# Attention: the product with the values in two halves of the queries, one behind each pair of score banks

## The chip, the cores and the metric

The kernel runs on one core of a Trainium2 chip. The metric is the device time of one execution in microseconds (us), the median of several; smaller is better. TensorE does the matrix products, VectorE (DVE) the reductions, ScalarE (ACT) the exponentials and copies, GpSimd (POOL) the masking of probabilities, and SyncE (SP) issues the transfers.

## What is computed

One transformer layer on x of shape 4 x 2048 x 256 in f32: causal attention with 16 heads of 16, then an MLP with ternary weights. The change touches the attention alone. Cut to that:

```python
def _L0_attn_ref(x, W_attn, b_attn, W_proj, b_proj):
    qkv = x @ W_attn + b_attn
    q, k, v = jnp.split(qkv, 3, axis=2)
    qh, kh, vh = (heads(q), heads(k), heads(v))          # b h s d, d = 16
    scores = jnp.einsum('bhqd,bhkd->bhqk', qh, kh) * scale
    causal = jnp.tril(jnp.ones((S, S), dtype=bool))
    scores = jnp.where(causal, scores, -jnp.inf)
    probs = jax.nn.softmax(scores, axis=-1)
    out = jnp.einsum('bhqk,bhkd->bhqd', probs, vh)
    out = out.transpose(0, 2, 1, 3).reshape(B, S, D)
    return out @ W_proj + b_proj

x = x + _L0_attn_ref(_layernorm(x), ...)
x = x + _L0_ffn_ref(_layernorm(x), ...)
```

## The kernel before

Four parts follow each other: build_prep (weights), build_qkv (norm and q, k, v to DRAM), build_attention, build_mlp. The attention takes the time from about 290 to 1763 us of the span and is the only part that changes.

**Units and steps.** A unit is one batch and one group of four heads; there are 16. In a unit the queries go in four chunks of 512. STEPS lists the work of a unit: in chunk c, 4c + 1 steps of one block (128 keys by 512 queries), then a double-block step (384 and 128 queries, two different key blocks at the diagonal), then a two-bank step (256 queries, two heads side by side in a bank). That makes 36 steps, 32 with four banks of scores (one a head) and 4 with two. Diagonal blocks are masked.

**What a step does.** TensorE writes the scores of a bank into `ps_s` (L961), a ring of three PSUM banks (BANKS = 3). A head pair lies in two row groups of the array: banks 0 and 2 use partitions 0 to 49 (r = 0), banks 1 and 3 partitions 64 to 113 (r = 1). ScalarE takes the exponential of each bank into `probs` (L848), a ring of six steps in SBUF. Three steps later (PV_BEHIND = 3) TensorE multiplies them with the values into `ps_acc` (L980), the four heads in four column groups of 32; each f32 product is two records in the trace, so a step's product shows as x8. The last matmul of a step's product signals pv_done; at the end of a chunk ScalarE copies `ps_acc` (L831) and signals acc_copied.

**Maxima.** The maximum of each query is needed as an extra row of q before its scores. It is found ahead of time (LEAD = 40 items): an item is a pair of matmuls into `ps_m` (L926), one in each row group, and one reduction on VectorE (L871, L874); there are two slots (SLOTS = 2). A unit has 68 items. Of the 20 at the diagonal, 8 have four mask products each and 12 have eight (L932, bf16, 128 columns). Once a chunk the maxima are parted on POOL (L774, L776), turned on TensorE into a bank of the ring (L939), copied on ScalarE (L823) and sent by SP into q.

**What sets the order.** Each engine runs its instructions in the order written, and `order(s, last)` (L112) lists the pieces of step s for all engines: banks, items, the turn ("rows") and the product ("values"). TensorE alone takes the "values" pieces from it. `await_bank` (L942) makes the scores of ring use k wait until ScalarE has read use k - 3. `values` (L965) waits for the masks of its step (L971) or its exponentials (L973), and at a chunk's start for the copy of the accumulator (L976).

Of the kernel before, what the change touches and what calls it, by code (L numbers as in the profile page):

```python
# [64 lines left out]
STEPS = [step for c in range(NCH) for step in  # L65
         [(c, 1, [(j, 0, 0, CH)]) for j in range(TT * c + 1)]
         + [(c, 1, [(TT * c + 1, P, 0, 3 * P), (TT * c + 3, 3 * P, 3 * P, P)]), (c, 2, [(TT * c + 2, 2 * P, 0, 2 * P)])]]
NS = len(STEPS)
CHUNK_END = [s + 1 for s in range(NS) if s + 1 == NS or STEPS[s + 1][0] > STEPS[s][0]]
CHUNK_START = [0] + CHUNK_END[:-1]  # L70
DIAGONALS = [s for s, (c, _, blocks) in enumerate(STEPS) if blocks[0][0] >= TT * c]
ND = len(DIAGONALS)
PV_BEHIND = 3


def banks_of(s):

    return GH // STEPS[s][1]
# [17 lines left out]
def items_at(x):  # L96

    y = x + LEAD  # L100
    got = [("item", (y >= NM, y % NM))]
    for what, z in (("found", y - 1), ("rows", y - ROWS_BEHIND)):
        if z >= 0 and z % NM + 1 in MAX_END:
            got.append((what, (z >= NM, MAX_END.index(z % NM + 1))))
    return got
# [6 lines left out]
def order(s, last):  # L112


    x = sum(banks_of(i) // 2 for i in range(s))
    if banks_of(s) == 4:
        got = [("bank", 0), ("bank", 1), *items_at(x), ("bank", 2), ("values", None), ("bank", 3), *items_at(x + 1)]
    else:
        got = [("bank", 0), ("bank", 1), ("values", None), *items_at(x)]
    return [(what, y) for what, y in got if not (last and what in ("item", "found", "rows") and y[0])]  # L120


def ring_uses(s, last):
# [15 lines left out]
def zero(n):  # L139

    return isinstance(n, int) and n == 0
# [460 lines left out]
def build_attention(nc, io, keep, scr):  # L602

    with ExitStack() as ctx:
# [26 lines left out]
        pv_done, loads_passed = t.sem("pv_done"), t.sem("loads_passed")  # L631
# [20 lines left out]
        def uses(n, u, by):  # L652

            return by * (n // 2 + 1) if isinstance(n, int) else by // 2 * (n + 2 - u)

        def halves(n, c):

            return 2 * n + c // 2
# [9 lines left out]
        def taken(n, k):  # L668

            return OPENED_ROWS + USES * n + k + 1  # L670
# [6 lines left out]
        def unit_of(x, n, u):  # L677

            return n + 1 if x[0] else n, 1 - u if x[0] else u, x[1]
# [232 lines left out]
        @block.tensor  # L912
        def _(pe):
            def form_max(n, par, k):
                c, pieces = MAXES[k]
                slot = k % SLOTS
                if not (isinstance(n, int) and NM * n + k < SLOTS):

                    pe.wait_ge(slot_freed, NM * n + k - SLOTS + 1)
                if k in [0] + MAX_END:  # L920

                    pe.wait_ge(stack_in[par][c], uses(n, par, 16 * STACK))
                for p, tt, i, col, width in pieces:
                    for r in range(2):
                        rows = slice(ROW * r, ROW * r + TERMS)
                        last = pe.matmul(ps_m[:, 2 * slot + r, col:col + width], qs[par][rows, c, p, tt * P:(tt + 1) * P],  # L926
                                         ks[par][rows, i, p, 0:width], start=True, stop=(i < c), skip_group_check=True)
                    if i == c:
                        for half in range(2):
                            for r in range(2):  # L930
                                rows = slice(ROW * r, ROW * (r + 1))
                                last = pe.matmul(ps_m[:, 2 * slot + r, col + width - P:col + width], ident_half[rows, half],  # L932
                                                 mask_half[rows, half], start=False, stop=(half == 1), skip_group_check=True)
                last.then_inc(slot_filled, 1)

            def turn_rows(n, c, k):

                pe.wait_ge(max_parted, 2 * NCH * n + 2 * (c + 1))
                pe.transpose(ps_s[0:MROWS * GH * TT, k % BANKS, 0:P],  # L939
                             max_parts[c % 2][:].bitcast(F32).rearrange("p r a x -> p (r a x)"), keep["ident"][:]).then_inc(ring_filled, 1)  # L940

            def await_bank(n, k, first):  # L942

                if k >= BANKS:
                    pe.wait_ge(ring_taken, taken(n, k - BANKS))
                elif not first:
                    pe.wait_ge(ring_taken, taken(n, -1 - (USES - 1 - k) % BANKS))
                elif k < OPENED_ROWS:
                    pe.wait_ge(ring_taken, k + 1)

            def scores(n, u, s, bank, k):
                c, heads, blocks = STEPS[s]
                if s in CHUNK_START and bank == 0:

                    pe.wait_ge(rows_in[c % 2], 16 * 2 * MROWS * (halves(n, c) + 1))
                for x in range(heads):
                    p, r = (bank + 2 * x) // 2, bank % 2
                    rows = slice(ROW * r, ROW * r + TERMS + MROWS)
                    for j, q0, col, width in blocks:
                        at = CH // heads * x + col  # L960
                        last = pe.matmul(ps_s[:, k % BANKS, at:at + width], ks[u][rows, j // TT, p, j % TT * P:(j % TT + 1) * P],  # L961
                                         qs[u][rows, c, p, q0:q0 + width], start=True, stop=True, skip_group_check=True)
                last.then_inc(ring_filled, 1)

            def values(n, u, s, last_unit):  # L965
                c, heads, blocks = STEPS[s]
                if s == 0:
                    pe.wait_ge(v_in[u], uses(n, u, 16))
                if s in DIAGONALS:
                    before = sum(len(STEPS[i][2]) for i in DIAGONALS if i <= s)  # L970
                    pe.wait_ge(probs_masked, MASKS * n + before)  # L971
                else:
                    pe.wait_ge(ring_taken, scores_taken(n, s, last_unit))  # L973
                if s in CHUNK_START and not (zero(n) and c == 0):

                    pe.wait_ge(acc_copied, NCH * n + c)  # L976
                for j, q0, col, width in blocks:
                    for h in range(GH):
                        at = h // banks_of(s) * (CH // heads) + col
                        last = pe.matmul(ps_acc[h * VW:(h + 1) * VW, q0:q0 + width], vs[u][:, j, h],  # L980
                                         probs[:, s % RING, h % banks_of(s), at:at + width],
                                         start=(j == 0), stop=(s + 1 in CHUNK_END), skip_group_check=True)
                last.then_inc(pv_done, 1)

            MASKS = sum(len(STEPS[i][2]) for i in DIAGONALS)
            pe.wait_ge(fixed_in, 16 * FIXED)
            opened = 0
            for what, x in OPENING:
                if what == "item":
                    form_max(0, 0, x[1])  # L990
                elif what == "rows":
                    turn_rows(0, x[1], opened)
                    opened += 1

            def body(n, u, first, last):
                k = 0
                for s in range(NS):
                    for what, x in order(s, last):
                        if what == "bank":
                            await_bank(n, k, first)  # L1000
                            scores(n, u, s, x, k)
                            k += 1
                        elif what == "item":
                            form_max(*unit_of(x, n, u))
                        elif what == "rows":
                            unit, _, c = unit_of(x, n, u)
                            await_bank(n, k, first)
                            turn_rows(unit, c, k)
                            k += 1
                        elif what == "values" and s >= PV_BEHIND:  # L1010
                            values(n, u, s - PV_BEHIND, last)
                        elif what == "values" and not first:
                            values(n - 1, 1 - u, NS + s - PV_BEHIND, False)
                if last:
                    for s in range(NS - PV_BEHIND, NS):
                        values(n, u, s, True)

            over_units(pe, body)


# [286 lines left out]
```

## Time and profile before

| | |
|---|---|
| median of 3 runs | 2255.41 us (2251.96 to 2268.09) |
| profiled execution | 2259.07 us, its span 2257.1 us |
| TensorE busy | 2076.8 us, 92% |
| VectorE busy | 1845.8 us, 82% |
| ScalarE busy | 1441.3 us, 64% |
| POOL busy | 469.2 us, 21% |

Shares of busy time are means over all four parts of the program. A matmul's end in the trace is modelled and matmuls overlap, so TensorE's busy share is no measure of how full it is; the distance between the starts of its instructions is. Times in the rows below are from the span's start.

### The profile page before, as it was taken

How to read it: one execution, taken by the hardware profiler on the slowest of the kernel's cores; microseconds unless marked ns; L12 is line 12 of the kernel's file. 1: busy time of each engine (PE TensorE's matmuls, PEld its weight loads, DVE VectorE, ACT ScalarE, POOL GpSimd, SP SyncE). 2: the span in 40 equal slices, each digit the busy share in tenths (PEclk: the TensorE clock that was granted, in tenths of full speed). 3: DMA queues.
4: the chain of work that ended last, by engine and by line, in shares of the span. 5: the costliest groups of instructions: out<-in, count | busy, mean ns of one | idle time of the engine just before them, and what ended most of it. 6: DMA issues, size and time to landing. Idle time of an engine off the chain costs nothing. (4 is left out here: it accounts for less than half of the span.)

```text
span 2257.1 us, 40453 instructions
## 1 busy us (share of the span) xinstructions
PE 2076.8 (92%) x15605; PEld 1216.2 (54%) x15605; DVE 1845.8 (82%) x2413; ACT 1441.3 (64%) x2768; POOL 469.2 (21%) x621
## 2 busy tenths in 40 slices
PE   3997699999999999999999999999999488888888
PEld 2886354444544545444444454454543277777777
DVE  7896888888888888888888888888881288787776
ACT  1332078787888878878888788787887243444444
POOL 0000011111110111101111111011110256666664
PEclk8998589999999999999999999999998599999999
DMA  2899321222222122222122212211210212222220
GB/s 90 325 372 333 66 47 54 68 62 57 59 61 75 44 54 68 58 68 51 54 65 58 63 53 66 75 45 54 67 41 11 89 45 69 75 75 75 75 75 29
DMA packets 162976, 184.69 MB, mean 82 GB/s; under 512 B 41936, under 2 KB 102880, under 8 KB 160736
## 3 DMA queue, kind: packets, MB, share of 16 engines
q1 hardware_dynamic: 154112, 174.50, 26.0%
q10 hardware_dynamic: 8672, 7.60, 1.1%
q8 instruction: 123, 2.02, 0.4%
q14 instruction: 69, 0.57, 0.1%
HBM read 104.16 MB, written 76.02 MB: 80 GB/s over the span
## 5 line engine op out<-in xcount | busy, mean ns | idle before, releaser
L848 ACT ACTIVATE probs<-ps_s 128x512 f32<-128x512 f32 x2176 | 1144.5, 602 | 302.8 <-PE ps_s L961 293.1
L871 DVE TENSOR_REDUCE maxes<-ps_m 128x2 f32<-128x1024 f32 (+1 forms) x960 | 1136.8, 1218 | 160.2 <-PE ps_m L926 105.9
L961 PE MATMUL ps_s<-qs,ks 50*128 50x512 f32 (+3 forms) x2560 | 805.9, 414 | 9.0 <-ACT probs L848 9.0
L926 PE MATMUL ps_m<-ks,qs 48*128 48x512 f32 (+3 forms) x2560 | 715.5, 426 | 35.0 <-DMA ks<-ones 23.9
L961 PEld LDWEIGHTS ps_s<-qs,ks 50*128 50x128 f32 x2560 | 402.8, 188 | 505.4 <-ACT probs L848 464.6
L980 PE MATMUL ps_acc<-probs,vs 128*32 128x512 f32 (+3 forms) x5120 | 594.3, 546 | 0.6
L926 PEld LDWEIGHTS ps_m<-ks,qs 48*128 48x128 f32 x2560 | 362.5, 190 | 125.1 <-issue 44.8
L786 POOL TENSOR_SCALAR_AFFINE_SELECT probs<-probs 128x512 f32<-128x512 f32 x256 | 157.0, 635 | 746.1 <-ACT probs L848 746.1
L1119 POOL TENSOR_TENSOR hid<-square,hid 128x512 fp32r<-128x512 f32 x128 | 196.2, 1554 | 184.7 <-DVE square L1144 174.4
L932 PE MATMUL ps_m<-mask_half,ident_half 64*128 64x128 bf16 x2048 | 207.3, 227 | 0.0
L980 PEld LDWEIGHTS ps_acc<-probs,vs 128*32 128x32 f32 x5120 | 109.2, 109 | 159.8 <-issue 94.2
L874 DVE TENSOR_REDUCE maxes<-ps_m 128x2 f32<-128x768 f32 (+1 forms) x256 | 161.7, 685 | 28.7 <-PE ps_m L932 28.2
L1144 DVE TENSOR_TENSOR square<-relu 128x512 f32<-128x512 f32 x128 | 134.9, 1074 | 58.5 <-ACT relu L1178 55.5
L1241 PE MATMUL ps_y<-w,hid 128*128 128x256 f32 x1024 | 140.8, 299 | 1.5 <-POOL hid L1119 1.4
L774 POOL CAST max_parts<-neg_max 128x16 fp32r<-128x16 f32 x64 | 12.6, 196 | 606.1 <-DVE neg_max L880 606.1
L1241 PEld LDWEIGHTS ps_y<-w,hid 128*128 128x128 f32 x1024 | 135.9, 206 | 2.2 <-POOL hid L1119 2.1
L1178 ACT ACTIVATE relu<-ps_h 128x512 f32<-128x512 f32 x128 | 76.2, 595 | 68.0 <-PE ps_h L158 59.0
L156 PE MATMUL ps_h<-mxn_t,w 128*128 128x512 f32 x256 | 105.2, 411 | 2.5 <-DVE mxn_t L434 1.4
L157 PE MATMUL ps_h<-mxn_t,w 128*128 128x512 f32 x256 | 103.3, 404 | 0.0
L932 PEld LDWEIGHTS ps_m<-mask_half,ident_half 64*128 64x128 bf16 x2048 | 94.7, 98 | 15.5 <-issue 5.5
L158 PE MATMUL ps_h<-mxn_t,w 128*128 128x512 f32 x256 | 101.8, 398 | 0.0
L1183 ACT ACTIVATE hid<-relu 128x512 fp32r<-128x512 f32 x128 | 81.0, 633 | 4.0
(126 smaller groups left out, 1589.6 us busy)
## 6 DMA issues: line engine op xcount, KB each, us to landing
qs<-q_scr SPq DMA_DIRECT2D x384, 64.0 KB, 2.7
ks<-k_scr SPq DMA_DIRECT2D x384, 64.0 KB, 2.7
q_scr<-parts SPq DMA_DIRECT2D x32, 512.0 KB, 4.0
k_scr<-parts SPq DMA_DIRECT2D x32, 512.0 KB, 5.5
v_scr<-v_out SPq DMA_DIRECT2D x16, 1024.0 KB, 7.4
vs<-v_scr SPq DMA_DIRECT2D x16, 1024.0 KB, 5.9
o_scr<-acc_sb SPq DMA_DIRECT2D x64, 256.0 KB, 2.9
o_in<-o_scr SPq DMA_DIRECT2D x32, 256.0 KB
```

What stands on the lines that cost most here:

```text
L156: pe.matmul(out, sh, mh, start=start, stop=False)
L786: pool.affine_select(out=tile, in_=tile, compare_op=ALU.is_ge, fill=0.0, base=0, pattern=[[0, GH], [1, P]], channel_multiplier=-1).then_in ...
L848: act.activation(probs[:, s % RING, x], ps_s[:, k % BANKS], ACT.Exp).then_inc(ring_taken, 1)
L871: last = dve.tensor_reduce(maxes[c % 2][:, :, pairs, tt, i], banks, AX.X, ALU.max)
L874: last = dve.tensor_reduce(maxes[c % 2][:, :, p, tt, i], ps_m[:, 2 * slot:2 * slot + 2, col:col + width], AX.X, ALU.max)
L926: last = pe.matmul(ps_m[:, 2 * slot + r, col:col + width], qs[par][rows, c, p, tt * P:(tt + 1) * P], ks[par][rows, i, p, 0:width], start=T ...
L932: last = pe.matmul(ps_m[:, 2 * slot + r, col + width - P:col + width], ident_half[rows, half], mask_half[rows, half], start=False, stop=(h ...
L961: last = pe.matmul(ps_s[:, k % BANKS, at:at + width], ks[u][rows, j // TT, p, j % TT * P:(j % TT + 1) * P], qs[u][rows, c, p, q0:q0 + widt ...
L980: last = pe.matmul(ps_acc[h * VW:(h + 1) * VW, q0:q0 + width], vs[u][:, j, h], probs[:, s % RING, h % banks_of(s), at:at + width], start=( ...
L1119: pool.tensor_tensor(hid[:, 1, m], square[:, m], hid[:, 0, m].bitcast(F32), ALU.subtract).then_inc(low_done, 1)
L1144: dve.tensor_tensor(square[:, m], relu[:, m], relu[:, m], ALU.mult).then_inc(square_done, 1)
L1241: last = pe.matmul(ps_y[:, i, (tt % 2) * DIM:(tt % 2 + 1) * DIM], hid[:, a, m, tt * P:(tt + 1) * P], keep["w2"][:, m], start=(m == 0 and a ...
```

## The change

In a four-bank step the order was: bank 0, bank 1, an item, bank 2, the product, bank 3, an item. It becomes: bank 0, bank 1, an item, the first half of the product, bank 2, bank 3, an item, the second half. The halves part the queries: 256 and 256 of a plain step's 512, 128 and 128 of a two-bank step's 256, and the 384 and the 128 of a double-block step. In a two-bank step both halves stand where the product stood. The waits stand before the first half, and pv_done is signalled by the second.

```diff
@@ order
     if banks_of(s) == 4:
-        got = [("bank", 0), ("bank", 1), *items_at(x), ("bank", 2), ("values", None), ("bank", 3), *items_at(x + 1)]
+        got = [("bank", 0), ("bank", 1), *items_at(x), ("values", 0), ("bank", 2), ("bank", 3), *items_at(x + 1), ("values", 1)]
     else:
-        got = [("bank", 0), ("bank", 1), ("values", None), *items_at(x)]
+        got = [("bank", 0), ("bank", 1), ("values", 0), ("values", 1), *items_at(x)]
...
+def halves_of(s):
+
+    blocks = STEPS[s][2]
+    j, q0, col, width = blocks[0]
+    if len(blocks) > 1:
+        return [blocks[:1], blocks[1:]]
+    return [[(j, q0, col, width // 2)], [(j, q0 + width // 2, col + width // 2, width // 2)]]
...
-            def values(n, u, s, last_unit):
-                c, heads, blocks = STEPS[s]
-                if s == 0:
+            def values(n, u, s, half, last_unit):
+                c, heads, _ = STEPS[s]
+                if s == 0 and half == 0:
                     pe.wait_ge(v_in[u], uses(n, u, 16))
-                if s in DIAGONALS:
+                if half == 0 and s in DIAGONALS:
                     before = sum(len(STEPS[i][2]) for i in DIAGONALS if i <= s)
                     pe.wait_ge(probs_masked, MASKS * n + before)
-                else:
+                elif half == 0:
                     pe.wait_ge(ring_taken, scores_taken(n, s, last_unit))
-                if s in CHUNK_START and not (zero(n) and c == 0):
+                if half == 0 and s in CHUNK_START and not (zero(n) and c == 0):
 
                     pe.wait_ge(acc_copied, NCH * n + c)
-                for j, q0, col, width in blocks:
+                for j, q0, col, width in halves_of(s)[half]:
                     for h in range(GH):
                         at = h // banks_of(s) * (CH // heads) + col
                         last = pe.matmul(ps_acc[h * VW:(h + 1) * VW, q0:q0 + width], vs[u][:, j, h],
                                          probs[:, s % RING, h % banks_of(s), at:at + width],
-                                         start=(j == 0), stop=(s + 1 in CHUNK_END), skip_group_check=True)
-                last.then_inc(pv_done, 1)
+                                         start=(j == 0 and half == 0), stop=(s + 1 in CHUNK_END), skip_group_check=True)
+                if half == 1:
+                    last.then_inc(pv_done, 1)
```

On TensorE a plain step (512 columns everywhere) read like this before; `ps_s` are scores, `ps_m` an item, `ps_acc` the product.

```order
L961 MATMUL ps_s<-qs,ks 128x512
L926 MATMUL ps_m<-ks,qs 128x512 x2
L961 MATMUL ps_s<-qs,ks 128x512 x2
L926 MATMUL ps_m<-ks,qs 128x512 x2
L961 MATMUL ps_s<-qs,ks 128x512
L980 MATMUL ps_acc<-probs,vs 32x512 x4
```

And now, the same step:

```order
L970 MATMUL ps_s<-qs,ks 128x512 x2
L935 MATMUL ps_m<-ks,qs 128x512 x2
L989 MATMUL ps_acc<-probs,vs 32x256 x4
L970 MATMUL ps_s<-qs,ks 128x512 x2
L935 MATMUL ps_m<-ks,qs 128x512 x2
L989 MATMUL ps_acc<-probs,vs 32x256 x4
```

The scores of bank 3 (the first row of before) have moved up beside those of bank 2, and each pair is followed by an item and half a product.

The end of a chunk on TensorE, from the product of the last four-bank step over the two-bank step (`128x256 x4`) to the next chunk, before:

```order
L980 MATMUL ps_acc<-probs,vs 32x512 x4
L961 MATMUL ps_s<-qs,ks 128x384
L961 MATMUL ps_s<-qs,ks 128x128
L926 MATMUL ps_m<-ks,qs 128x256 x2
L932 MATMUL ps_m<-mask_half,ident_half 128x128 x4
L926 MATMUL ps_m<-ks,qs 128x256 x2
L932 MATMUL ps_m<-mask_half,ident_half 128x128 x4
L961 MATMUL ps_s<-qs,ks 128x256 x4
L980 MATMUL ps_acc<-probs,vs 32x512 x4
L926 MATMUL ps_m<-ks,qs 128x512 x2
L961 MATMUL ps_s<-qs,ks 128x512 x2
```

And now:

```order
L970 MATMUL ps_s<-qs,ks 128x384
L970 MATMUL ps_s<-qs,ks 128x128
L970 MATMUL ps_s<-qs,ks 128x384
L970 MATMUL ps_s<-qs,ks 128x128
L935 MATMUL ps_m<-ks,qs 128x256 x2
L941 MATMUL ps_m<-mask_half,ident_half 128x128 x4
L935 MATMUL ps_m<-ks,qs 128x256 x2
L941 MATMUL ps_m<-mask_half,ident_half 128x128 x4
L989 MATMUL ps_acc<-probs,vs 32x256 x4
L970 MATMUL ps_s<-qs,ks 128x256 x4
L989 MATMUL ps_acc<-probs,vs 32x256 x8
L935 MATMUL ps_m<-ks,qs 128x512 x2
```

The item with its eight mask products now stands between the pieces of a whole pair of scores and half a product, and in the two-bank step the halves touch (x8).

## Rows read from the trace of the kernel before

**Rows 1.** The page's busy times (us, share of the span, instructions).
```profile
PE 2076.8 (92%) x15605; PEld 1216.2 (54%) x15605; DVE 1845.8 (82%) x2413; ACT 1441.3 (64%) x2768; POOL 469.2 (21%) x621
```

**Rows 2.** Windows view, one unit: us; busy of PE, PEld, DVE, ACT, POOL; clock; DMA.
```profile
836.60:928.50 91.90, 91.64 (x775) 44.57 (x772) 81.51 (x85) 73.89 (x145) 11.45 (x24) 1.00 0.21 60
```

**Rows 3.** Timeline of ScalarE, copies a unit apart: start, length, line, operation, shapes, count, idle.
```profile
849.99 0.60 ACT L848 ACTIVATE probs<-ps_s 128x512 f32<-128x512 f32 x1
850.48 0.58 ACT L831 COPY acc_sb<-ps_acc 128x512 f32<-128x512 f32 x1
...
942.33 0.58 ACT L831 COPY acc_sb<-ps_acc 128x512 f32<-128x512 f32 x1
```

**Rows 4.** Groups by form in one unit (836.6 to 928.5): busy us, mean ns, idle before.
```profile
L871 DVE TENSOR_REDUCE maxes<-ps_m 128x2 f32<-128x1024 f32 x57 | 67.6, 1218 | 8.2 <-PE ps_m L926 7.2 <-PE ps_m L932 0.8
...
L932 PE MATMUL ps_m<-mask_half,ident_half 64*128 64x128 bf16 x128 | 13.0, 222 | 0.0
```

**Rows 5.** Timeline of TensorE in a plain step.
```profile
908.35 1.06 PE L980 MATMUL ps_acc<-probs,vs 128*32 128x512 f32 x8
909.35 0.50 PE L961 MATMUL ps_s<-qs,ks 50*128 50x512 f32 x1
909.35 0.73 PE L926 MATMUL ps_m<-ks,qs 48*128 48x512 f32 x2
...
909.93 0.63 PE L926 MATMUL ps_m<-ks,qs 48*128 48x512 f32 x2
910.53 0.49 PE L961 MATMUL ps_s<-qs,ks 50*128 50x512 f32 x1
910.96 1.06 PE L980 MATMUL ps_acc<-probs,vs 128*32 128x512 f32 x8
```

**Rows 6.** Timeline of ScalarE: the exponential of the scores of 909.35.
```profile
909.88 0.60 ACT L848 ACTIVATE probs<-ps_s 128x512 f32<-128x512 f32 x1 [0.54 <-PE ps_s L961]
```

**Rows 7.** Timeline of TensorE behind a two-bank step's product.
```profile
859.35 0.50 PE L926 MATMUL ps_m<-ks,qs 48*128 48x512 f32 x2
859.69 0.40 PE L961 MATMUL ps_s<-qs,ks 50*128 50x512 f32 x2
859.92 0.39 PE L926 MATMUL ps_m<-ks,qs 48*128 48x512 f32 x2
860.16 0.39 PE L961 MATMUL ps_s<-qs,ks 50*128 50x512 f32 x1
860.47 1.07 PE L980 MATMUL ps_acc<-probs,vs 128*32 128x512 f32 x8
```

**Rows 8.** Timeline of TensorE in a two-bank step, up to its product.
```profile
857.41 0.44 PE L961 MATMUL ps_s<-qs,ks 50*128 50x384 f32 x1
...
857.75 0.68 PE L961 MATMUL ps_s<-qs,ks 50*128 50x256 f32 x4
858.36 0.64 PE L980 MATMUL ps_acc<-probs,vs 128*32 128x512 f32 x4
```

**Rows 9.** Timeline of TensorE: a product of 256 columns and the next scores.
```profile
848.88 0.64 PE L980 MATMUL ps_acc<-probs,vs 128*32 128x256 f32 x8
849.45 0.50 PE L961 MATMUL ps_s<-qs,ks 50*128 50x512 f32 x1
```

**Rows 10.** Timeline of TensorE: ends of two stretches with masked items.
```profile
872.06 0.50 PE L961 MATMUL ps_s<-qs,ks 50*128 50x512 f32 x1
...
873.75 1.06 PE L980 MATMUL ps_acc<-probs,vs 128*32 128x512 f32 x8
...
877.60 0.50 PE L961 MATMUL ps_s<-qs,ks 50*128 50x512 f32 x1
...
879.46 1.06 PE L980 MATMUL ps_acc<-probs,vs 128*32 128x512 f32 x8
```

**Rows 11.** Timeline of TensorE: a stretch with a turn of the maxima.
```profile
887.89 0.49 PE L926 MATMUL ps_m<-ks,qs 48*128 48x512 f32 x2
...
889.43 0.64 PE L980 MATMUL ps_acc<-probs,vs 128*32 128x512 f32 x4
```

More of the change, by code:

```diff
@@ L1010, in body @@
                         elif what == "values" and s >= PV_BEHIND:
-                            values(n, u, s - PV_BEHIND, last)
+                            values(n, u, s - PV_BEHIND, x, last)
                         elif what == "values" and not first:
-                            values(n - 1, 1 - u, NS + s - PV_BEHIND, False)
+                            values(n - 1, 1 - u, NS + s - PV_BEHIND, x, False)
                 if last:
                     for s in range(NS - PV_BEHIND, NS):
-                        values(n, u, s, True)
+                        for half in range(2):
+                            values(n, u, s, half, True)
             over_units(pe, body)
```

## The prediction

> **What bounds the kernel now.** The page comes first: TensorE is busy for 92% of the span [rows 1]. The windows view of one unit of attention says more: VectorE works 81.51 of 91.90 us and ScalarE 73.89, while the 91.64 of TensorE count overlapping, modelled matmuls as busy [rows 2], so that number can't tell a full TensorE from one that waits. A unit lasts 91.85 us, from one copy of the accumulator (L831) to the same copy a unit later [rows 3]; 16 units are 1470 of the 2257.1 us. VectorE's 67.6 us of large reductions in a unit [rows 4] leave it some 10 us short of the unit: it is the next bound, not this one.
>
> The timeline of a plain step (four banks, two plain items) shows the bound [rows 5]. From product (908.35) to product (910.96) it takes 2.61 us. The product itself holds TensorE 1.00 us (908.35 to 909.35). The stretch from there to the next product is 1.61. In it the scores of bank 2 start at 910.53, 0.60 after the matmuls of 909.93, where others start 0.23 apart. They wait for ScalarE: ring slot k takes the scores of k, and k-3 must have been read. For bank 2 that is bank 3 of the step before, whose scores began at 909.35, whose exponential began at 909.88 and took 0.60 [rows 6]. So there is a loop: scores of bank 3, exponential, scores of bank 2 (1.18 to 1.19 later), 0.42 to the product, 1.00 of product, scores of bank 3 again: 2.61. How long would the stretch be without it? The stretch after a two-bank step has seven matmuls of 512 columns, in four slots of paired row groups as a plain step has, and takes 1.12 [rows 7]. The wait is thus worth 1.61 - 1.12 = 0.49 in a plain step.
>
> **A ledger of the unit before.** It has 32 four-bank and 4 two-bank steps. Content without waits: 32 stretches of 1.12; four of 0.95, that of a two-bank step (857.41 to 858.36) [rows 8]; 32 products of 1.00 and 4 of 256 columns at 0.57 [rows 9]. Masks: 128 mask products in a unit [rows 4], in 12 items of eight and 8 of four by the code. A stretch with two items of eight takes 1.86 (877.60 to 879.46), one with an eight and a four 1.69 (872.06 to 873.75) [rows 10]; against 1.12 this is 0.37 for an item of eight and 0.20 for one of four. Turning the maxima (L939) makes a stretch 1.54 (887.89 to 889.43) [rows 11], 0.42 more, four times. Sum: 35.8 + 3.8 + 32.0 + 2.3 + 4.4 + 1.6 + 1.7 = 81.6. The unit takes 91.85, so 10.2 us are waits, nearly all the one above. That is also where masks hide now: a stretch with one item of four has 1.32 of content and fits under 1.61.
>
> **What the change does, part by part.**
>
> 1. Bank 2 and bank 3 are now neighbours, and half a product stands after each pair. The half cycle is: scores pair, item, half product. The first pair after a product takes 0.34 to the next, the last 0.31 to the product (859.35 to 859.69, 860.16 to 860.47) [rows 7]: 0.65. Half a product is the 256-column one, 0.57 [rows 9]. Sum 1.22, a plain step 2.44. Does the ring allow it? The second score of a pair now needs the exponential of the first score of the pair before: the same 1.19, against 1.22. The wait is gone with 0.03 to spare. A plain step gains 0.17.
> 2. The price in every step: splitting a product costs 2 x 0.57 - 1.00 = 0.14, and going from scores to product and back twice costs 2 x 0.65 - 1.12 = 0.18. In the two-bank steps the halves touch, and the split costs 0.05 (0.14 less the 0.09 of one switch). First the row: the first pair after a product needs 0.34 where others need 0.23 [rows 7]. The Trainium skill (TensorEngine Tiling (Array Packing), Key Properties) says that changing the tiling mode drains the engine; scores use row groups and the product column groups, so this rule speaks against the change. It gives no figure. Were the drain free, the 32 x 0.18 = 5.8 us of a unit would go; I keep them, since both sides of the 256-column product show the full switch.
> 3. Stretches: the 64 half cycles have 60 x 0.65, and 4 after a two-bank step 0.88 (one more pair, 0.23); the two-bank stretches 4 x 0.71 (its four pieces to the product 0.61 [rows 8], and 0.10 for being first): 45.3. Products: 34.3 + 32 x 0.14 + 4 x 0.05 = 39.0. The second product half signals pv_done, and ScalarE's ring of six steps is three away: nothing.
> 4. Masks 6.0 and turns 1.7 as before, but now with no wait to hide in: the spare is 0.03 a half.
> 5. Scores in pieces: each of the four double-block steps has 4 pieces in place of a pair, twice. Bounds: 0 (hidden in the other row group) and 0.30 (four pieces 0.61 [rows 8] against a pair 0.31). I take 0.20: 8 x 0.20 = 1.6.
> 6. New waits. A half with a 128-column product (0.57 - 0.21 = 0.36, by the 0.43 that 256 columns cost) lasts 1.01 and then waits for the ring until 1.19: 0.18, some 6 times without masks, 1.1. The copy of the accumulator: the last half of a chunk's last product now ends a step, ScalarE copies it behind the exponential of bank 3 (0.58 for the copy [rows 3]), and the next chunk's first half comes one half cycle later, not one step: scores of that step at 1.01 after bank 2's, product wanted at 1.66, copy done at 0.53 + 2 x 0.49 (one exponential or copy to the next [rows 3]) + 0.58 = 2.1. That is 0.5 once, and where masks lengthen the half some 0.1: 0.7 together. A turn takes a ring slot between two pairs, so that bank 3 waits for the exponential of bank 1: 0.15 x 4 = 0.6. Bounds of all: 0.5 and 4.
>
> POOL's masks and SP's queue keep their order; the product waits for masks three steps old. VectorE is busy 81.51 for the 68 items of a unit [rows 2], 1.20 an item, against halves of 1.22 and more: it still hides, and is late next if the halves get shorter.
>
> Sum after: 45.3 + 39.0 + 6.0 + 1.7 + 1.6 + 2.4 = 96.0 us, against 91.85: **+4.1 a unit, +66 in 16 units**. The profiled execution has 2259.07 us, the median is 3.7 below: 2325 less 4, **about 2320 us**, 2.9% slower. In short: 0.17 is won in the plain steps, fewer than half of all, and each masked step of two eights goes from 2.86 to 2.44 + 0.74 = 3.18.
>
> **Rivals.** The forecast has 66%.
>
> A, faster: what is hidden today stays hidden. An all-plain unit would take 32 x 2.61 and four times 0.95 + 1.12 + 0.57 - 1.61 = 1.03, that is 87.6 us, so masks, turns and pieces add only 4.2 today. If that stays, the unit is 84.3 + 4.2 = 88.5 (84.3 is the first two sums of step 3), and the kernel 2255 - 54 = 2201. It turns at 91.85 - 84.3 = 7.5 us of exposed extras; I count 11.7. For it: two row groups run side by side. Against it: the unstalled 1.86 of two masked items [rows 10]. 12%.
>
> B, within 1%: masks cost their streaming alone. A pair of 512 columns takes 0.23, so a pair of mask products (128 columns) 0.06: 0.24 and 0.12 for items of eight and four, 3.8 a unit and not 6.0; then 93.8, +31. With the pieces free as well (bound 0), 92.2: +6, 2261. The Trainium skill (the same section) has different tiles execute weight loads and matmuls in parallel, which is this case; rows 10 show no sign of it where the loads are many. 16%, around 2270.
>
> C, much slower: the 0.03 of spare isn't there. If the second score of a pair loads its weights late, 0.1 in each of some 44 unmasked halves is 4.4 a unit, 70 more: 2390. 6%.
>
> At the bounds of the terms: if the new waits are at 4 and the pieces at 0.30, the unit is 98.4 and the kernel 2360. It is the upper end of the forecast's own 66%, of which most lies between 2285 and 2352.
>
> The edit can hardly fail to do what it says, since the order on TensorE is written out.
>
> **Numbers.** Range 2256 to 2352: it holds the forecast and B, and leaves out A, C and the outermost of the bounds. A change of 1% is 22.5 us, about what a measurement can tell. Faster by over 1%: A, 0.12. Within: B, 0.16. Slower: the forecast and C, 0.72.
>
> **What would show it.** Plain steps of 2.44 between like halves, without the 0.60 gap before scores: step 1. Half products 0.57 apart from the next scores: step 2. Stretches of scores and an item of eight at 1.02: step 4. A gap of half a microsecond before the first product of a chunk: step 6. A unit (copy to copy) of 96.0. I am wrong if plain steps stay at 2.6 (C), or masked halves are about as short as plain ones (A).

## The result, and the profile after

| | before | after |
|---|---|---|
| median us, 20 runs each | 2262.49 (2249.91 to 2276.22) | 2276.94 (2260.49 to 2288.98) |
| ratio, 95% interval | | 1.0061 (1.0031 to 1.0090) |
| profiled execution, its span | 2259.07, 2257.1 | 2287.96, 2286.2 |
| one unit, copy to copy | 91.87 | 92.98 |

The kernel became slower by 0.6%, about 14 us, where 2.9%, some 65 us, were forecast. The sign was right, the size more than four times too large.

The unit is the better measure: within one execution it repeats to 0.1 us in most units (those of the changed kernel behind the first lie between 93.0 and 93.8), while whole executions of either kernel scatter by over 1%. Two copies of the accumulator, one unit apart, from ScalarE's timeline after the change (before: [rows 3]):

```profile
1323.45 0.57 ACT L840 COPY acc_sb<-ps_acc 128x512 f32<-128x512 f32 x1
...
1416.43 0.57 ACT L840 COPY acc_sb<-ps_acc 128x512 f32<-128x512 f32 x1
```

16 units of +1.1 us are +18 us, inside the interval of the ratio (7 to 20 us). The two profiled executions differ by 29; 7 of the other 11 us lie in the first unit, where the granted clock was 0.50 of full in one execution and 1.00 in the other. The windows view of 300 to 315 us, of before:

```profile
300.00:315.00 15.00, 15.00 (x115) 6.51 (x114) 13.49 (x14) 12.19 (x25) 2.44 (x4) 1.00 0.45 80
```

and of after (the clock is the third number from the end):

```profile
300.00:315.00 15.00, 15.00 (x96) 5.81 (x96) 7.35 (x6) 7.34 (x14) 2.49 (x4) 0.50 0.38 80
```

Executions of one and the same kernel differ in the granted clock as well: twenty of the changed kernel had means over the span from 0.945 to 0.960, and took 2289 us at the lower and 2260 at the higher. So these 7 us aren't put down to the change. One execution of each kernel was profiled, so whether the clock always differs at this place isn't shown.

**A plain step**, TensorE's timeline after, which answers to [rows 5]:

```profile
927.73 0.64 PE L989 MATMUL ps_acc<-probs,vs 128*32 128x256 f32 x8
928.30 0.51 PE L970 MATMUL ps_s<-qs,ks 50*128 50x512 f32 x2
928.64 0.40 PE L935 MATMUL ps_m<-ks,qs 48*128 48x512 f32 x2
928.98 0.64 PE L989 MATMUL ps_acc<-probs,vs 128*32 128x256 f32 x8
929.54 0.50 PE L970 MATMUL ps_s<-qs,ks 50*128 50x512 f32 x2
929.88 0.40 PE L935 MATMUL ps_m<-ks,qs 48*128 48x512 f32 x2
930.21 0.64 PE L989 MATMUL ps_acc<-probs,vs 128*32 128x256 f32 x8
```

From 927.73 to 930.21 it takes 2.48 us, against 2.61. The gap of 0.60 before the scores of bank 2 is gone. Half a product holds TensorE 0.57 (927.73 to 928.30), the pair and the item 0.67 (928.30 to 928.98).

**Masked items.** Two halves with items of eight mask products, which answer to [rows 10]:

```profile
882.65 0.50 PE L970 MATMUL ps_s<-qs,ks 50*128 50x512 f32 x2
...
883.17 0.29 PE L941 MATMUL ps_m<-mask_half,ident_half 64*128 64x128 bf16 x4
...
883.64 0.64 PE L989 MATMUL ps_acc<-probs,vs 128*32 128x256 f32 x8
884.21 0.50 PE L970 MATMUL ps_s<-qs,ks 50*128 50x512 f32 x2
```

The stretch is 0.99 (882.65 to 883.64), 0.32 more than the plain 0.67; a half is 1.56 and two are 3.11, where such a step took 2.86. What the plain steps win is lost here. With an item of four the stretch is 0.80, 0.13 more:

```profile
888.67 0.50 PE L970 MATMUL ps_s<-qs,ks 50*128 50x512 f32 x2
...
889.47 0.64 PE L989 MATMUL ps_acc<-probs,vs 128*32 128x256 f32 x8
```

**The chunk's start**, with the copy of the accumulator:

```profile
863.34 0.43 PE L989 MATMUL ps_acc<-probs,vs 128*32 128x128 f32 x8
863.70 0.58 PE L970 MATMUL ps_s<-qs,ks 50*128 50x512 f32 x2
...
864.84 0.64 PE L989 MATMUL ps_acc<-probs,vs 128*32 128x256 f32 x8 [0.32 <-ACT acc_sb L840]
```

The stretch is 1.14 instead of 0.67: the first product of the chunk waits for ScalarE's copy.

**The two-bank step** ([rows 8]) and **a turn of the maxima** ([rows 11]):

```profile
871.93 0.50 PE L970 MATMUL ps_s<-qs,ks 50*128 50x256 f32 x4
872.37 1.07 PE L989 MATMUL ps_acc<-probs,vs 128*32 128x256 f32 x16
873.37 0.50 PE L935 MATMUL ps_m<-ks,qs 48*128 48x512 f32 x2
...
874.27 0.64 PE L989 MATMUL ps_acc<-probs,vs 128*32 128x256 f32 x8
...
894.71 0.50 PE L970 MATMUL ps_s<-qs,ks 50*128 50x512 f32 x2
...
895.36 0.29 PE L948 MATMUL ps_s<-ident,max_parts 128*32 128x128 f32 x1
895.58 0.64 PE L989 MATMUL ps_acc<-probs,vs 128*32 128x256 f32 x8
```

The four pieces of the two-bank step are at the product in 0.44; two touching halves take 1.00, as much as the whole product did. This turn stands in a four-bank step, directly ahead of a half product; its stretch is 0.87, 0.20 more than a plain one. So it is for two of the four turns of a unit. The other two belong to two-bank steps and stand between an item and scores, as all four did before:

```profile
902.84 0.49 PE L935 MATMUL ps_m<-ks,qs 48*128 48x512 f32 x2
903.26 0.28 PE L948 MATMUL ps_s<-ident,max_parts 128*32 128x128 f32 x1
903.48 0.50 PE L970 MATMUL ps_s<-qs,ks 50*128 50x512 f32 x2
...
904.15 0.64 PE L989 MATMUL ps_acc<-probs,vs 128*32 128x256 f32 x8
```

This stretch is 1.31, where the same one without a turn takes 0.90 (873.37 to 874.27): 0.40 more. And a double-block step's scores in pieces, 0.72 to the product:

```profile
898.82 0.51 PE L970 MATMUL ps_s<-qs,ks 50*128 50x384 f32 x4
899.17 0.45 PE L935 MATMUL ps_m<-ks,qs 48*128 48x512 f32 x2
899.54 0.64 PE L989 MATMUL ps_acc<-probs,vs 128*32 128x256 f32 x8
```

### The profile page after: what moved, and what is told of

Its sections match the earlier page's. It is cut to its first block and busy times, and to the rows that moved or that the text cites. A ratio compares the mean times of both kernels' runs of the same rounds, so it can differ in the third digit from the quotient of the medians.

```text
span 2286.2 us, 48645 instructions
## 1 busy us (share of the span) xinstructions
PE 2103.6 (92%) x19701; PEld 1175.8 (51%) x19701; DVE 1870.6 (82%) x2413; ACT 1478.3 (65%) x2768; POOL 470.9 (21%) x621
## 5 line engine op out<-in xcount | busy, mean ns | idle before, releaser
L857 ACT ACTIVATE probs<-ps_s 128x512 f32<-128x512 f32 x2176 | 1181.3, 596 | 296.4 <-PE ps_s L970 272.5
L880 DVE TENSOR_REDUCE maxes<-ps_m 128x2 f32<-128x1024 f32 (+1 forms) x960 | 1151.3, 1221 | 157.0 <-PE ps_m L935 98.3
L989 PE MATMUL ps_acc<-probs,vs 128*32 128x256 f32 (+2 forms) x9216 | 711.2, 386 | 11.7 <-ACT acc_sb L840 11.1
L970 PE MATMUL ps_s<-qs,ks 50*128 50x512 f32 (+3 forms) x2560 | 577.2, 454 | 0.0
L935 PE MATMUL ps_m<-ks,qs 48*128 48x512 f32 (+3 forms) x2560 | 525.3, 401 | 35.4 <-DMA ks<-ones 24.3
L970 PEld LDWEIGHTS ps_s<-qs,ks 50*128 50x128 f32 x2560 | 253.1, 188 | 420.1 <-ACT probs L857 392.1
L989 PEld LDWEIGHTS ps_acc<-probs,vs 128*32 128x32 f32 x9216 | 190.9, 109 | 306.6 <-issue 201.0
L935 PEld LDWEIGHTS ps_m<-ks,qs 48*128 48x128 f32 x2560 | 263.5, 192 | 78.7 <-DVE maxes L880 29.8
L941 PE MATMUL ps_m<-mask_half,ident_half 64*128 64x128 bf16 x2048 | 147.3, 227 | 0.0
L941 PEld LDWEIGHTS ps_m<-mask_half,ident_half 64*128 64x128 bf16 x2048 | 63.0, 98 | 71.6 <-issue 66.6
```

Of the source, the lines that this page charges most:

```text
L857: act.activation(probs[:, s % RING, x], ps_s[:, k % BANKS], ACT.Exp).then_inc(ring_taken, 1)
L880: last = dve.tensor_reduce(maxes[c % 2][:, :, pairs, tt, i], banks, AX.X, ALU.max)
```

## The experiments

**Theory 1** is the prediction's: before, a plain step waited for the ring loop, and that wait hid masks, turns and pieces; the change ends the wait and exposes them, and adds switches. **Theory 2**: halves cost by their split and switches alone, masks weigh the same in both kernels. **Theory 3**: TensorE or VectorE, and not the ring, set the plain step before. **Theory 4**: it is the pairing of the scores that shortens the step, the halves only cost. Unit lengths are medians over the units between the same copies of the profiled execution; ratios are to the kernel before on the same chip.

| run | unit us | median us | ratio (95%) |
|---|---|---|---|
| e1 before, no mask products | 89.75 | 2228.79 | 0.9857 (0.9793 to 0.9921) |
| e2 after, no mask products | 89.56 | 2218.56 | 0.9787 (0.9732 to 0.9843) |
| e3 split only | 92.07 | 2266.45 | 1.0013 (0.9976 to 1.0049) |
| e4 mixture | 91.59 | 2245.58 | 0.9917 (0.9882 to 0.9952) |
| e5 before, half exponentials | 89.07 | 2220.03 | 0.9776 (0.9731 to 0.9822) |
| e6 after, half exponentials | 91.44 | 2244.45 | 0.9884 (0.9836 to 0.9932) |
| e7 after, copy early | 93.13 | 2276.57 | 1.0036 (1.0005 to 1.0066) |
| e8 mixture 2 | 91.43 | 2255.97 | 0.9936 (0.9904 to 0.9968) |
| e9 whole product between | 101.13 | 2416.47 | 1.0654 (1.0573 to 1.0736) |
| e10 mixture 3 | 90.82 | 2236.25 | 0.9887 (0.9826 to 0.9948) |

### Are the masks what is exposed? (e1, e2)

The same edit on the kernel before (e1) and on the changed one (e2), in form_max:

```diff
-                                         ks[par][rows, i, p, 0:width], start=True, stop=(i < c), skip_group_check=True)
-                    if i == c:
+                                         ks[par][rows, i, p, 0:width], start=True, stop=True, skip_group_check=True)
+                    if False:
```

> The kernel before, without the mask products (L932) in the items of maxima; the maxima then run over whole blocks, everything else is the same. Theory 1 (what the ring wait of ScalarE hid in the kernel before, the masks above all, is exposed by the change): only what masked stretches last beyond 1.61 us goes, about 2.2 us a unit: unit 91.86 -> about 89.7, time some 35 us less. Theory 2 (the two halves cost by their split and second switch alone, masks weigh the same in both kernels): the masks' whole 4.8 us goes from here too: unit about 87.

> The changed kernel, without the mask products of the maxima. Theory 1: all of the masks' time goes (12 x 0.315 + 8 x 0.13 = 4.8 us a unit, less some ring waits that come back): unit 93.0 -> about 88.5, and so this kernel is faster than the kernel before without masks, by some 1.2 us a unit or 19 us. Theory 2: it stays about 1.1 us a unit slower than the kernel before without masks.

Measured: 91.87 to 89.75 in the kernel before, 2.1 us a unit, as theory 1 had it. In the changed kernel 93.0 to 89.6, 3.4 us. So the masks weigh 1.3 us a unit more in the changed kernel, and without them the change no longer slows a unit: 89.56 against 89.75. More than that can't be read from the two, as the units of e2 lie between 89.1 and 90.3. Theory 1's sign holds, theory 2 falls. The size was off: 4.5 was expected in e2. The masks had covered waits there as well. The chunk start of e2 at 749 us:

```profile
747.35 0.58 PE L970 MATMUL ps_s<-qs,ks 50*128 50x512 f32 x2
...
748.49 0.64 PE L989 MATMUL ps_acc<-probs,vs 128*32 128x256 f32 x8 [0.32 <-ACT acc_sb L840]
```

This stretch of 1.14 now stands at three chunk starts of a unit. In the changed kernel the second of them held an item of four and took 1.03, and the third an item of eight and took about the 0.99 of any such stretch.

### Does the split cost by itself? (e3)

```diff
-        got = [("bank", 0), ("bank", 1), *items_at(x), ("values", 0), ("bank", 2), ("bank", 3), *items_at(x + 1), ("values", 1)]
+        got = [("bank", 0), ("bank", 1), *items_at(x), ("bank", 2), ("values", 0), ("values", 1), ("bank", 3), *items_at(x + 1)]
```

> One part alone: the order of the kernel before, with the two halves of the product one behind the other where the whole product stood (bank 2, half 0, half 1, bank 3). Theory 1: without a switch between them the split costs nothing (1.001 against 0.996 in the two-bank steps of the changed kernel): unit 91.9, no change. Theory 2: more and narrower matmuls cost by themselves; the product is part of the ring loop, so 0.05 to 0.14 in each of 32 steps: unit 93.5 to 96.

Unit 92.07, time unchanged within its interval. Twice as many matmuls of half the width cost 0.2 us a unit when they follow each other. The 0.14 a step that the split costs in the changed kernel is thus not the number of matmuls; what is left is the second passage between scores and product, that is, between row groups and column groups.

### Was it the ring loop? (e5, e6)

In both kernels the exponential, with probs set to a constant at the start:

```diff
+            pool.memset(probs[:], 1.0)
...
-                            act.activation(probs[:, s % RING, x], ps_s[:, k % BANKS], ACT.Exp).then_inc(ring_taken, 1)
+                            act.activation(probs[:, s % RING, x, 0:256], ps_s[:, k % BANKS, 0:256], ACT.Exp).then_inc(ring_taken, 1)
```

> The kernel before, with each exponential over 256 of the 512 columns of its bank (the other columns of probs keep a constant set at the start, so half of the probabilities aren't computed). It shortens the ring loop and nothing on TensorE. An exponential of 0.60 us becomes about 0.37. Theory 1 (the loop scores, exponential, scores, product, sets the plain step before): plain step 2.61 -> about 2.38, unit 91.86 -> 87.5 to 88.5. Theory 3 (TensorE itself or VectorE sets it): unit stays near 91.9.

> The changed kernel with the same half exponentials (half of the probabilities aren't computed). Theory 1 (the change has left the ring loop behind, and its plain steps of 2.48 are TensorE's own time: two switches and eight half matmuls more): plain step stays 2.46 to 2.48, only the waits behind short products and copies go: unit 93.0 -> 91 to 91.8, so this kernel is now some 3 us a unit slower than the kernel before with half exponentials. Theory 3 (its halves still wait for the ring): plain step falls below 2.4, and the unit with it to about 89.

TensorE's timeline of e5, a plain step:

```profile
1250.48 0.50 PE L962 MATMUL ps_s<-qs,ks 50*128 50x512 f32 x1
...
1251.45 0.50 PE L962 MATMUL ps_s<-qs,ks 50*128 50x512 f32 x1
1251.88 1.07 PE L981 MATMUL ps_acc<-probs,vs 128*32 128x512 f32 x8
1252.88 0.50 PE L962 MATMUL ps_s<-qs,ks 50*128 50x512 f32 x1
```

And ScalarE's, the exponential of the scores of 1250.48:

```profile
1251.01 0.38 ACT L849 ACTIVATE probs<-ps_s 128x256 f32<-128x256 f32 x1 [1.04 <-PE ps_s L962]
```

The exponential became 0.22 shorter (0.60 to 0.38), and the step with it, 2.61 to 2.40 (1250.48 to 1252.88): the scores of bank 2 follow those of bank 3 after 0.97 instead of 1.18. Theory 3 falls for the kernel before. In the changed kernel the plain step went from 2.48 to 2.45 only, so the change had all but left the loop behind. From e6:

```profile
1291.10 0.64 PE L990 MATMUL ps_acc<-probs,vs 128*32 128x256 f32 x8
...
1293.55 0.64 PE L990 MATMUL ps_acc<-probs,vs 128*32 128x256 f32 x8
```

Its unit lost 1.5, against 2.8 before: the 0.03 a plain step, the waits behind short products and turns, and part of those for the copy. With half exponentials the change costs 2.4 us a unit (91.44 against 89.07); some 3 was expected. The unit of e5, 89.07, was expected at 88.5 at most; the steps that stay longer are the masked ones and those where VectorE's slots are late (3.2 us of TensorE's waits in a unit are put down to it, 1.3 before).

### Are the halves needed? (e9)

On the kernel before:

```diff
-        got = [("bank", 0), ("bank", 1), *items_at(x), ("bank", 2), ("values", None), ("bank", 3), *items_at(x + 1)]
+        got = [("bank", 0), ("bank", 1), *items_at(x), ("values", None), ("bank", 2), ("bank", 3), *items_at(x + 1)]
```

> One part alone: banks 2 and 3 side by side as in the change, but the product whole, behind the first pair and its item (bank 0, bank 1, item, product, bank 2, bank 3, item). Theory 1 (a pair of scores needs the exponential of the pair before, 1.19 us after its start; the halves matter because each fills that time): first half 0.65 + 1.00, second half without a product waits for the ring until 1.19, plain step 2.84, unit 97 to 99. Theory 4 (pairing the scores is what shortens the step, one switch less is better still): plain step 2.48 minus the 0.32 of split and switch, below 2.3, or VectorE's 2.36; unit below 91.

```profile
1378.23 0.50 PE L961 MATMUL ps_s<-qs,ks 50*128 50x512 f32 x2
1378.57 0.39 PE L926 MATMUL ps_m<-ks,qs 48*128 48x512 f32 x2
1378.81 0.39 PE L961 MATMUL ps_s<-qs,ks 50*128 50x512 f32 x1
1379.42 0.50 PE L961 MATMUL ps_s<-qs,ks 50*128 50x512 f32 x1 [0.23 <-ACT probs L848]
1379.42 0.73 PE L926 MATMUL ps_m<-ks,qs 48*128 48x512 f32 x2
1380.08 1.06 PE L980 MATMUL ps_acc<-probs,vs 128*32 128x512 f32 x8
1381.08 0.50 PE L961 MATMUL ps_s<-qs,ks 50*128 50x512 f32 x2
```

The step is 2.85 (1378.23 to 1381.08), as worked out. The second score of the pair stands at 1379.42, 1.19 after the pair of 1378.23, and 0.61 behind its partner of 1378.81. Theory 4 falls. The unit of 101.1 is 2 above what was expected.

### Can the new waits be taken away? (e7)

On the changed kernel: the product of a two-bank step whole in the first half's place, and the copy behind the exponential of bank 2.

```diff
+    if STEPS[s][1] == 2:
+        return [blocks, []]
...
+                            if x == 2 and (at := ended(s, PV_BEHIND, n, first)):
+                                copy_acc(*at)
```

> The changed kernel, with the 256-column product of a chunk's last step left whole in the first half's place, and ScalarE's copy of the accumulator moved from behind the exponential of bank 3 to behind that of bank 2. Theory 1 (the stall of 0.47 us before a chunk's first product comes from this copy, and half products of 128 columns cost ring waits): unit 93.0 -> 91.3 to 92, no stretch of 1.14 left at a chunk's start. Rival: the ring takes it back (the half without a product waits 0.5 for ScalarE), unit 93.

The rival was right: unit 93.13. The half without a product waits for the ring:

```profile
762.43 0.64 PE L995 MATMUL ps_acc<-probs,vs 128*32 128x256 f32 x8
763.00 0.50 PE L974 MATMUL ps_s<-qs,ks 50*128 50x512 f32 x2
...
764.18 0.50 PE L974 MATMUL ps_s<-qs,ks 50*128 50x512 f32 x1 [0.22 <-ACT probs L859]
764.18 0.73 PE L939 MATMUL ps_m<-ks,qs 48*128 48x512 f32 x2
764.85 0.64 PE L995 MATMUL ps_acc<-probs,vs 128*32 128x256 f32 x8
```

1.18 from 763.00 to 764.18: any half with less than about 0.5 of product behind it (1.18 less 0.67) meets the ring. No stretch of 1.14 is left at a chunk's start, as theory 1 had it, but the two stretches without a product between them take as much back.

### The new order only where it pays (e4, e8, e10)

e4 takes the new order where both items of a step are unmasked, else both halves behind bank 2. e8 also leaves out steps with a short product. e10 takes it only from the fifth step of the last chunk on, and keeps products whole elsewhere. The core, of e10:

```diff
+LIMIT = 1
+FROM = CHUNK_START[3] + 4
...
-    if banks_of(s) == 4:
+    if banks_of(s) == 4 and (s < FROM or extras_at(x) + extras_at(x + 1) >= LIMIT):
         got = [("bank", 0), ("bank", 1), *items_at(x), ("bank", 2), ("values", None), ("bank", 3), *items_at(x + 1)]
+    elif banks_of(s) == 4:
+        got = [("bank", 0), ("bank", 1), *items_at(x), ("values", 0), ("bank", 2), ("bank", 3), *items_at(x + 1), ("values", 1)]
```

extras_at(x) is above zero where the item has mask products.

> The new order only in four-bank steps whose two items are both unmasked; in the others the two halves stand together behind bank 2, as the product did before. Theory 1: the plain steps keep their 2.48 (against 2.61) and the masked ones go back to what they were (2.85 instead of 3.11): unit about 90.5, about 20 us or 1% faster than before. Theory 2: a unit no shorter than 91.9.

> The new order only in four-bank steps with two unmasked items and a full product of 512 columns; the order of before (both halves together behind bank 2) in masked steps and in those whose product is short (256 columns, or 384 and 128). Theory 1 (before, a short product shortens the ring loop itself, so halves win nothing there and add waits and a copy stall): unit 91.6 of the first such mixture -> 90.0 to 90.5, about 1.2% faster than before. Rival: each change from one order to the other costs a ring wait that eats the gain: unit 91.3 or more.

> The new order only in the plain steps late in a chunk of 16 blocks (last chunk, from its fifth step, unmasked items), everything else word for word as before, products whole. Theory 1: those seven steps take 2.48 instead of 2.61 and nothing else moves but one change of order and back: unit 90.8 to 91.1, about 0.7% faster than before. Rival: the changes of order and the new place of the product cost as much again: unit 91.4 or more, as in the two mixtures so far.

The first two missed: 91.59 and 91.43, where 90.5 and 90.0 to 90.5 were expected. Counted from exponential to exponential, the plain steps have their 2.48 in both, but the steps at a chunk's start got longer: the first step after a two-bank step from 2.26 to 2.64 (step 3 of a unit) and the first one with a full product again from 2.28 to about 2.66 (step 6). In e4 this is no price of changing order: it has the new order from step 3 to step 8, and the changed kernel, which never changes order, has 2.64 and 2.67 there as well. By chunk, in us (medians of the same count):

| | chunk 0 | chunk 1 | chunk 2 | chunk 3 |
|---|---|---|---|---|
| before | 6.82 | 16.76 | 28.94 | 39.34 |
| after | 7.08 | 17.08 | 29.88 | 38.97 |
| e4 | 7.09 | 17.08 | 29.06 | 38.38 |
| e8 | 6.86 | 17.01 | 29.19 | 38.36 |
| e10 | 6.82 | 16.76 | 28.94 | 38.30 |

The whole gain of the mixtures, about 1.0 us a unit, lies in the last chunk, where the run of plain steps is long, and even the changed kernel wins 0.4 there. In the short chunks the new order costs, about 0.3 in each of the first two, where no item has mask products. e8, which takes the old order for short products, has four more changes of order in a unit; it wins the 0.3 back in chunk 0, not in chunk 1, and loses 0.1 more in chunk 2. Whether the changes themselves cost isn't shown. e10 leaves the short chunks alone, changes order once a unit and back, in the long run of plain steps, and hit: its unit, from the copies, is 90.81.

```profile
1288.84 0.57 ACT L852 COPY acc_sb<-ps_acc 128x512 f32<-128x512 f32 x1
...
1379.65 0.57 ACT L852 COPY acc_sb<-ps_acc 128x512 f32<-128x512 f32 x1
```

At a ratio of 0.9887 (0.9826 to 0.9948) it is the fastest version with the whole computation, better than both kernels. By the units alone it would be 17 us, 0.7%; the interval holds that, and the rest of the measured 1.1% isn't explained by the change.

## Why the prediction was wrong

**What held.** The bound: ScalarE's ring loop set the plain step (e5, e9). Step 1: the plain step fell to 2.48, forecast 2.44. The ring had not quite 0.03 to spare: of the 0.02 by which each half is longer, e6 without the ring's wait gives back more than half. Step 2: products were forecast at 39.0 us in a unit and took 38.7. Step 3, the stretches, forecast 45.3 and took 45.5, but by luck: 60 halves of 0.67 and not 0.65 are 1.2 more, and the two-bank step's pieces at 0.44 and not 0.71 are 1.1 less. Step 6, new waits: forecast 2.4 and found 2.3, of other parts: those for the copy 1.0 (forecast 0.7, with 0.47 at one chunk's start where 0.5 was written), those behind products of 128 columns about 0.8 (1.1), and those after a turn 0.5 (0.6), at two of the four turns and 0.21 and 0.28 long, where 0.15 at each was written. And the direction held.

**What failed: steps 4 and 5.** Masks, turns and pieces were forecast at 6.0 + 1.7 + 1.6 = 9.3 us a unit, and took 4.8 + 1.2 + 0.4 = 6.4. These 2.9 us are nearly all of the 3.0 by which the unit was over-forecast (of the others, products were 0.3 and waits 0.1 less, stretches 0.2 more). These costs are read from the stretches of one unit; only the masks were also taken away (e1, e2), and there part of their time came back as waits.

- Masks (1.2 too much): 0.37 and 0.20 were read from the order of before, less a plain 1.12. There a matmul of scores in one row group starts together with one of the maxima in the other; now both of a pair are of one kind. In the new order an item of eight costs 0.32 (0.99 less 0.67) and one of four 0.13 (0.80 less 0.67): 12 x 0.315 + 8 x 0.13 = 4.8. Rival B's price by streaming alone, 3.8, was too low by about as much (1.0) as mine was too high.
- Turns (0.5 too much): 0.42 was read from [rows 11], where the turn stands between an item and scores:

```profile
888.31 0.28 PE L939 MATMUL ps_s<-ident,max_parts 128*32 128x128 f32 x1
888.53 0.50 PE L961 MATMUL ps_s<-qs,ks 50*128 50x512 f32 x2
```

  It has the product's shape of array (128*32 in both), so there it passes from one shape to the other and back by itself. Now the two turns in four-bank steps stand directly ahead of a half product and cost 0.20; the two in two-bank steps stand as before and cost 0.40 (read from the one at 903.26; the stretch of the other, 1.63, also holds a wait for the copy). The shape in the row and the place in the new order would have told.
- Pieces (1.2 too much): the bound of 0.30 came from the 0.61 in [rows 8], where a matmul of the maxima started together with the first piece (857.75):

```profile
857.75 0.44 PE L926 MATMUL ps_m<-ks,qs 48*128 48x512 f32 x1
```

  By themselves four pieces take 0.44, and a double-block pair 0.05 more than a plain one (0.72 less 0.67), where 0.20 was written. The same 0.61 stands in step 3, in the two-bank stretches.

**Why so little an error cost so much.** The unit was forecast at 96.0 and took 93.0, 3% off. But the answer was the difference of two such sums, 4.1 forecast and 1.1 found. The prices written down for the masks (3.8 and 6.0) and the bounds of the pieces (0 and 2.4) held the outcome between them, and together they span more than the answer. For the masks the upper end was taken; yet with the middle of both (4.9 and 1.2) the unit would be 94.5, still +2.6. The rest was the turns, and the pieces, which lay near their lower bound. Rival B, at 16%, had the better number (2270 against 2277), in part by luck, since its price of the masks was too low and it kept the turns and pieces too dear; and the range held the time.

**What stays open.** That masks cost 0.05 to 0.07 an item less in the new order was seen in two traces; why was not tested by itself. The same holds for the two prices of a turn and for the 0.61 of the pieces. The scatter of whole executions goes with their mean granted clock; it was not tested either. And the price of the new order in short chunks (0.3 in each of the first two) is measured but not taken apart.

## What to carry to other kernels

A wait on a loop hides whatever else stands in the same stretch; before it is taken away, sum what it hides, and expect the gain only in stretches that hide nothing. Here the same edit loses 0.6% everywhere and wins some 0.7% (by the unit) when confined to the long run of plain steps. A cost read as the difference of two stretches holds for that neighbourhood only: look which array shape and row group stand on either side before carrying it over, and when the forecast is a small difference of large sums, compare it with the width of the bounds of its terms: here that was wider than the forecast itself.

## What was not expected of the hardware

- Eight matmul records of 256 columns and eight more right behind them hold TensorE 1.00 us, as long as eight of 512 (1.00); half of them alone holds it 0.57. The extra 0.14 appears only where scores stand between the halves (e3: 0.2 us in a whole unit where they touch).
- TensorE's granted clock stood at 0.50 of full, the 1.2 GHz level, in every profiled execution from 240 to 255 us, where the first maxima are found ahead of the first unit, and rose to full between 285 and 345 us at a moment that differed between executions. In the profiled execution of before TensorE had been busy for 12.80 us of 15 from 270 to 285, and the clock was full from 300 on. Between the two executions shown above the later rise makes about 7 us of the first unit. The last unit of the attention, the first without items of maxima, took 92.98 and 93.97 in the two kernels, and between 73.8 and 103.9 over the ten experiments.
